# The scaling product of the feed-forward quantiser, moved from VectorE to GpSimd in two pieces, with the rounding as a step of its own

## The reference

```python
def _quantize_mx(x, ebits, mfrac, emax_elem, max_norm):
    xb = x.reshape(shp[:-1] + (shp[-1] // BLOCK, BLOCK))
    amax = jnp.max(jnp.abs(xb), axis=-1, keepdims=True)
    sexp = jnp.floor(jnp.log2(jnp.where(amax == 0, 1.0, amax))) - emax_elem
    sexp = jnp.clip(sexp, -SCALE_EMAX, SCALE_EMAX)
    scale = jnp.exp2(sexp)
    q = _quantize_elem(xb / scale, ebits, mfrac, max_norm) * scale
...
gate = _mx_linear(x, w_gate)
up = _mx_linear(x, w_up)
inter = jax.nn.silu(gate) * up
return _mx_linear(inter, w_down)
```

## Time and profile before

| | |
|---|---|
| median of three runs | 485.39 us (479.9, 485.39, 485.39) |
| the profiled execution: its time | 480.16 us |
| its span, first to last instruction | 478.3 us |
| mean granted TensorE clock, share of full speed | 0.921 |
| busy: TensorE, VectorE, ScalarE, GpSimd | 77%, 75%, 39%, 33% |

### The profile page before, as it was taken

How to read it: one execution, slowest core, us unless ns; L and a number is a source line. 1 busy time by engine, 2 the same in 40 slices (tenths; PEclk the granted TensorE clock), 3 DMA queues, 4 the chain that set the end, 5 groups by cost and what they waited for, 6 DMA issues and landing times.

```text
span 478.3 us, 6936 instructions
## 1 busy us (share of the span) xinstructions
PE 367.9 (77%) x2330; PEld 248.8 (52%) x2330; DVE 359.5 (75%) x857; ACT 188.4 (39%) x331; POOL 155.6 (33%) x147
## 2 busy tenths in 40 slices
PE   7899788999999678957948888977656488650764
PEld 4576456545568457846635565656533156430333
DVE  4588348685549999699796667569995986789895
ACT  4456427233232204412354354533005488540331
POOL 4019400087416325554325413123412110031240
PEclk9999999899999879999979999999888789976687
DMA  8900000032120222234973911824000760000001
GB/s 281 254 28 1 10 1 2 0 112 84 48 67 14 75 89 88 89 88 115 227 123 82 172 56 46 131 57 56 0 1 0 122 122 1 2 0 6 18 19 47
DMA packets 33713, 32.67 MB, mean 68 GB/s; under 512 B 3876, under 2 KB 32784, under 8 KB 33680
## 3 DMA queue, kind: packets, MB, share of 16 engines
q1 hardware_dynamic: 31088, 28.99, 26.1%
q0 software_dynamic: 992, 1.68, 1.1%
q10 hardware_dynamic: 1600, 1.57, 1.0%
HBM read 28.04 MB, written 4.19 MB: 67 GB/s over the span
## 4 chain that ended last, share of the span: by engine, by line
PE 45%; DVE 31%; issue 12%; ACT 8%; POOL 3%; DVEq 0%; ACTq 0%; POOLq 0%
PE bank L870 10%; PE bank L782 5%; PE bank L896 5%; PE bank L755 3%; PE bank L798 3%; PE bank L1006 2%; PE bank L970 2%; DVE mxraw L1624 2%; DVE x L1458 2%; DVE mam L1466 2%; DVE probs L1551 2%; PE bank L766 2%; PE bank L918 2%; PE bank L832 1%; ACT probs L1078 1%
## 5 line engine op out<-in xcount | busy, mean ns | idle before, releaser
L870 PE MATMUL bank<-tok_r,probs_r 128*128 128x512 f32 x104 | 46.6, 448 | 17.4 <-DVE wT L1447 9.7
L896 PE MATMUL bank<-wexp,wT 128*128 128x256 f32 x192 | 53.5, 403 | 6.0 <-DVE x L1458 5.9
L1128 ACT ACTIVATE silu_sb<-bank 128x512 f32<-128x512 f32 x32 | 19.1, 598 | 79.3 <-PE bank L870 79.3
L673 POOL TENSOR_TENSOR wexp_r<-wexp,probs_r 128x1024 fp32r<-128x1024 f32 x13 | 31.3, 2409 | 48.1 <-ACT probs_r L1089 48.1
L1325 DVE TENSOR_SCALAR probs<-probs,hi 128x512 f32<-128x512 f32 x64 | 35.0, 599 | 14.8 <-ACT probs L1078 14.7
L591 POOL TENSOR_TENSOR mx_grid<-parts,bl 128x1024 bf16<-128x1024 fp8e4 x9 | 17.2, 1908 | 88.5 <-DVE parts L1627 88.5
L1078 ACT ACTIVATE probs<-bank 128x1024 f32<-128x1024 f32 x32 | 32.2, 1026 | 29.8 <-PE bank L782 29.8
L896 PEld LDWEIGHTS bank<-wexp,wT 128*128 128x128 f32 x192 | 36.6, 200 | 13.1 <-issue 6.7
L1551 DVE SCALAR_TENSOR_TENSOR probs<-bank,dexp 128x384 f32<-128x384 f32 x48 | 26.5, 555 | 21.2 <-PE bank L956 15.3
L870 PE MATMUL bank<-tok_r,wexp_r 128*128 128x512 f32 x104 | 41.7, 401 | 0.0
L576 POOL TENSOR_TENSOR mxraw<-mxraw,mx_grid 128x512 f32<-128x512 f32 x12 | 15.3, 1278 | 69.6 <-DVE mx_grid L1492 69.6
(11 more groups left out here) (261 smaller groups left out, 891.1 us busy)
## 6 DMA issues: line engine op xcount, KB each, us to landing
wexp<-in_L_ffn_W SPq DMA_DIRECT2D x28, 256.0 KB, 4.0
krep<-part_dram SPq DMA_DIRECT2D x32, 128.0 KB, 5.3
qrep<-part_dram SPq DMA_DIRECT2D x32, 128.0 KB, 4.8
wexp<-in_L_ffn_Wg SPq DMA_DIRECT2D x14, 256.0 KB, 4.3
part_dram<-parts POOLq DMA_DIRECT2D x4, 384.0 KB, 3.0
part_dram<-parts SPq DMA_DIRECT2D x4, 384.0 KB, 2.6
x<-in_x ACTq DMA_DIRECT2D x2, 512.0 KB, 7.2
ctx<-in_ctx SPq DMA_DIRECT2D x2, 512.0 KB, 6.9
```

What stands on the lines that cost most here:

```text
L673: gp.tensor_tensor(low, raw, w_high[k % 2].bitcast(F32), ALU.subtract).then_inc(s["w_low_ready"], 1)
L870: mm = pe.matmul(bank[:, bk, :], lhs, rhs, start=(kk == 0 and q == 0), stop=(kk == KC - 1 and q == len(terms) - 1))
L896: mm = pe.matmul(bank[:, 2 + pair, D * t:D * t + D], hid[k % 2][m][:, col:col + P], wexp[:, k % WR, 2, m, :], start=(m == 0), stop=(m == 1))
L1128: act.activation(silu_sb[:, w % 2, :], bank[:, 0, :], ACT.Silu if direct else ACT.Tanh, scale=1.0 if direct else 0.5).then_inc(s["sigmoid_ ...
```

## The change

The multiplication with the inverse scale leaves VectorE. GpSimd does it, as two instructions over 512 columns each, once VectorE has signalled the inverse scale (new semaphore `q_inverse`); the second piece signals `q_scaled`. The rounding, which waits for that, and GpSimd's multiplication with the scale become a step `round` with a place of its own in the plan. In `stage_d` it stands between the first and the second `product` of the next stage. For quantise 0 it stands behind `accumulate` of steps 30 and 31.

```diff
-    plan += st("out", 30, 31) + st("quantise", 0) + st("accumulate", 30, 31)
+    plan += st("out", 30, 31) + st("quantise", 0) + st("accumulate", 30, 31) + st("round", 0)
...
-        return [now("last", 4, True) + early, part(0), part(1) + late, now("quantise", 0) + now("down", 3, True)]
+        return [now("last", 4, True) + early, part(0) + now("round", 1), part(1) + late, now("quantise", 0) + now("down", 3, True)]
...
             def quantise(k):
+                gp.wait_ge(s["q_inverse"], k + 1)
+                if k >= 1:
+                    gp.wait_ge(s["q_rounded"], k)
+                src = q_source(k)
+                for c in range(0, 1024, PIECE):
+                    m = gp.tensor_tensor(b3(q_tmp[:, c:c + PIECE]), b3(src[:, c:c + PIECE]), blocks(bl[:, k % 2, 2, c // 32:(c + PIECE) // 32]),
+                                         ALU.mult)
+                m.then_inc(s["q_scaled"], 1)
+
+            def round_(k):
...
-                seq.add(v.tensor_scalar(bl[:, b, 2, :].bitcast(I32), bl[:, b, 1, :].bitcast(I32), -1.0, float(0x7F000000 - (4 << 23)),
-                                        ALU.mult, ALU.add))
+                v.tensor_scalar(bl[:, b, 2, :].bitcast(I32), bl[:, b, 1, :].bitcast(I32), -1.0, float(0x7F000000 - (4 << 23)),
+                                ALU.mult, ALU.add).then_inc(s["q_inverse"], 1)
                 seq.add(v.tensor_scalar(bl[:, b, 3, :], bl[:, b, 1, :], 16.0, None, ALU.mult))
-                seq.wait()
-                seq.add(v.tensor_tensor(b3(q_tmp), b3(src), blocks(bl[:, b, 2, :]), ALU.mult))
+
+            def round_(k):
+                b = k % 2
+                v.wait_ge(s["q_scaled"], k + 1)
                 seq.wait()
                 lim = 7.5 / 64
                 v.tensor_scalar(q8[:, b, :], q_tmp, lim, -lim, ALU.min, ALU.max, saturate=False).then_inc(s["q_rounded"], 1)
```

More of the change, by code:

```diff
@@ L92 @@
 SPLIT_FROM = 3
+PIECE = 512
 SILU_STEPS = (3, 4, 5, 6, 7, 8, 14, 15)
@@ L405, in flamingo_layers @@
             e_done d_done qk_done c_done pvc_done pvc_copied t3_done h_placed h_centred h_squared h_scaled
-            mx_scaled q_rounded q_ready last_q_ready q_turned xqt_copied gu_done sil_done inter_ready it_copied dn_done x_final out_stored
+            mx_scaled q_inverse q_scaled q_rounded q_ready last_q_ready q_turned xqt_copied gu_done sil_done inter_ready it_copied dn_done x_final out_stored
             v_seq a_seq g_seq""".split()
@@ L691, in cell_in @@
                                  lsc[:, :].unsqueeze(1).broadcast_to([P, TH, D]), ALU.mult).then_inc(s["h_scaled"], 1)
-            steps = dict(w_split=w_split, x_split=x_split, mx_quantise=mx_quantise, q_split=q_split, cell_in=cell_in, quantise=quantise)
+            steps = dict(w_split=w_split, x_split=x_split, mx_quantise=mx_quantise, q_split=q_split, cell_in=cell_in, quantise=quantise, round=round_)
             for name, i in plan:
@@ L1647, in _ @@
                          cell_normalise=cell_normalise, cell_in=cell_in, cell_mid=cell_mid, cell_out=cell_out,
-                         quantise=quantise, product=product, last=last)
+                         quantise=quantise, round=round_, product=product, last=last)
             for name, i in plan:
```

## The result

In 20 runs of each kernel the change took the median from 484.86 to 487.85 us, 0.6% more. Ratios in this document are of the runs in the fast state alone, while the profiles of e5_round3_late, e8_one_piece, e10_round3_again and e12_before_again are of runs in a slow one, over 1.5% above the fastest of their kernel and with a granted clock of 0.883 to 0.894. The ratio is 1.0074, its 95% interval [1.0051, 1.0097]: 0.7% slower in this comparison. A second comparison of the same two kernels, with ten runs of the changed one (e4_again), gave medians of 487.38 against 485.89 us and a ratio of 0.9961 [0.9908, 1.0014]. So the timing settles that the difference is under 2%, and not how large it is or on which side. The forecast was 487 and +3.2 us (0.7%). The profiled execution took 486.79 us, its span is 485.1, its mean granted clock 0.909.

A forecast was written before the change was run, and what follows sets the result against it. VectorE's stream was taken to bound the tail, latency quantise 0, 4 and 9. Terms 0.86 + 0.50 - 0.31 + 0.86 + 0.41 + 0.86 gave +3.2 us; weighing 488.6 twice and 483.3 once gave 487, range 480.5 to 493.

The forecast's parts named there:

- Quantise 0, +0.86: At quantise 0, accumulate fills VectorE's wait, but the scale-back and all after it come 0.86 us later.
- Quantise 1 and 2, +0.50: In the middle, two exposed paths partly covered by each first product: 0.15 + 0.09 + 0.27, so +0.50 us.
- Quantise 3, -0.31: At quantise 3, a shorter lock wait gains 1.72 us; late rounding costs 0.61 and L1481's wait 0.81: -0.31 net.
- Quantise 4, +0.86: Latency-bound quantise 4 comes 0.86 us later; quantise 5's own path hides behind the wait for its successors.
- Quantise 6 to 9, +0.41: Three tail stages from quantise 6 to 9 take 16.71 us in place of 16.30: +0.41.
- the period of 5.57: Length in us of each tail stage after the change, as one loop through VectorE and GpSimd, with small gaps.
- The 0.09 of waiting: In each tail stage, L1481 would wait 0.09 us for the port lock held by GpSimd's scale-back.
- Quantise 9, +0.86: At quantise 9 nothing but a last is left to overlap, so the longer path costs 0.86 us.
- the lower price: Both GpSimd pieces at 1.91 us in place of 2.10, -0.19 at each of eight exposed places: sum +1.7 us.
- The relief counts: Rival, 7%: pieces hidden under other work, stages 1, 2, 5 to 8 each gain 1.26 us; about 480 us.
- TensorE's clock rises sooner: Rival, 15%: moved q_turn 3 and down 1 raise the clock before quantise 4's gate_up, saving 1.5 us: +1.7, 485.5.
- Slow pieces: Rival, 12%: each GpSimd piece takes 2.22 us, adding 2.3 at each of eight places: +22 us, 507.

The follow-up runs named there:

- e5_round3_late: Kernel before, every product still on VectorE, but quantise 3 rounded and scaled back late, behind cell_out and ahead of the last normalisation; ratio 0.9938 to the kernel before.
- e8_one_piece: Changed kernel with GpSimd's product as one instruction of 1024 columns in place of two of 512; ratio 1.0054 to the kernel before.
- e10_round3_again: Second run of the kernel before with only quantise 3 rounded and scaled back late, no product moved to GpSimd; ratio 0.9999 to the kernel before.
- e12_before_again: The kernel before itself, unaltered, profiled and timed once more; ratio 1.0016 to the kernel before.
- e1_front: Kernel before with the change made for quantise 0, 1 and 2 alone; ratio 1.0054 to the kernel before.
- e6_after_both: Changed kernel with the rounding put behind the second product of the next stage, so both products precede it; ratio 1.0109 to the kernel before.
- e3_tail: Kernel before with the change made for quantise 4 to 9 alone; ratio 1.0023 to the kernel before.
- e2_third: Kernel before with the change made for quantise 3 alone; ratio 0.9867 to the kernel before.
- e11_third_again: Second run of the kernel before with the change made for quantise 3 alone; ratio 0.9972 to the kernel before.

## Why the prediction was right, point by point

The forecast's sum was met by the first comparison (+3.2 against +3.0 between the medians and +3.29 over A, B and C). The second pair of profiles, e4_again against e12_before_again, has -0.87 in A, +0.07 in B and +1.33 in C, in all +0.53, and their medians differ by 1.5. So that the total came out to 0.2 us is luck. The mechanism held: longer paths at exposed places, and a saved 1.26 us of VectorE that turn mostly into waiting. The sizes of its points:

1. *Quantise 0, +0.86.* The path from L1633 to the rounding was 2.17 (356.54 to 358.71), with the `accumulate` steps in it as said; +0.79 by the same row of before.
2. *Quantise 1 and 2, +0.50.* Too much. From the maxima of quantise 1 to those of 2 came +0.07 for the 0.24 of the working (5.29 to 5.36), and from the inverse of quantise 2 to the end of the second product +0.18 for 0.27 (3.27 to 3.45). The rest of A lies within the spread of A, between 64.11 and 66.45 in the eight profiles whose front is unchanged (mean 65.36) and between 65.58 and 67.08 in the five with it changed (after, e1_front, e4_again, and with the variations of e6_after_both and e8_one_piece; mean 66.36). That is +1.0 where points 1 and 2 together said +1.36, with a spread that doesn't resolve it. Most of the +2.92 between the two first profiles is no sure part of the change; the part of the 0.70 clock above stays open.
3. *Quantise 3, -0.31.* Right in mechanism: L1580 waits for the second piece and L1481 for the late scale-back. But B gained 0.76, and where the cell values were slow it lost 0.07 to 0.12, which the point didn't allow for. In the first case all three of its terms were a little off, on the same side. L1582, behind the waiting L1580, starts 4.05 after the maxima in place of 5.98, so -1.93 where -1.72 was said. The late rounding lengthens the way from the last normalisation (L1278, L1265 before) to the maxima of quantise 4 from 1.41 to 1.89, +0.48 for +0.61. L1481 grew from 0.18 to 0.86, +0.68 for +0.81. Two of the three have one reason: a held tensor_scalar ends 0.03 to 0.04 after GpSimd's instruction (L1567 of before: 421.27 after 421.24; L1580: 425.75 after 425.71; L1481 in e6_after_both: 466.16 after 466.13). So its own 0.17 to 0.18 lie under the wait and don't follow it, as I had counted them.
4. *Quantise 4, +0.86.* From the inverse of quantise 4 to the maxima of quantise 6 it was 11.43 in both profiles of before, 11.96 after and 12.23 in e4_again: +0.53 to +0.80. Where this `gate_up` took 3.60 us on both sides, as in e4_again, the difference is +0.80; the 0.27 less is the clock's (below). Quantise 5's own path was hidden, as said.
5. *Quantise 6 to 9, +0.41.* This was wrong, in sign as well: 16.30 and 16.31 before, 16.09 after and in e4_again, -0.2. The step that failed is the period of 5.57. Measured it is 5.36, three times over in after and e4_again, and 5.35 to 5.37 in e3_tail. The 0.09 of waiting were not there: L604 ends at 462.99, L1481 starts at 462.89 and takes its usual 0.18. That fits the reason of point 3, by which so short a wait lies within the instruction. The path is 2.17 and not 2.24, and the "small gaps" were not there. Fully exposed, the stages are 0.2 shorter than VectorE's own stream was with a `last` in it (5.56, 5.57), and longer by 0.19 than the one without it (5.17). That "DVE's saved 1.23 us per stage turns wholly into waiting" is nearly right: in a stage with a `last` 1.09 of wait stand for the 1.26 of the product that went. In the stage without one the wait is 1.49, more than was saved.
6. *Quantise 9, +0.86.* From its maxima to the last `last` 9.27 before and 10.08 after, 9.74 and 10.50 in the second profiles: +0.81 and +0.76.

So the tail was put too high (+2.13, measured +1.13 and, between the second profiles, +1.33) and the gain at quantise 3 too low, by 0.45; and an excess in A that the points don't explain made up the rest. The total is right partly because its errors had both signs. The lower end of the range, 480.5, is also not what it was said to be: the lower price, +1.7, on 479.9 or 480.16 gives 481.6 to 481.9.

The rivals. *The relief counts* is out: the steps would have had to be near 4.3. *TensorE's clock rises sooner* is out as priced, 1.5 us, but not in kind. Quantise 4's `gate_up`, for which the earlier trace rows had a clock of 0.50, ran some 6.4 us later in the profile after, and its stretch there has 0.57:

```profile
451.50:455.00 3.50, 3.46 (x11) 1.39 (x12) 0.90 (x2) 0.68 (x2) 0.48 (x1) 0.57 0.05 16
```

Its eight matmuls took 3.34 us there and 3.60 in before and e4_again; the eight of `down` behind them 1.04, 1.92 and 1.37. That gave back 0.27 us in this execution and nothing in e4_again. In e2_third and e11_third_again, where `q_turn` 3 and `down` 1 stand nearer to it, 0.68 and 0.61 up to the maxima of quantise 6.

*Slow pieces* is out with 1.045 to 1.050 us for all twenty; beside them VectorE runs `last` and a `product`, which read one operand from PSUM. The range, 480.5 to 493, held the median.

## What to carry to other kernels

Work moved to an idle engine saves nothing where the moving engine then has too little to do under the hand-over: set the other engine's time plus both hand-overs (here 2.17 us) against what is left in the stream up to the first reader (here 1.1), and count exposed places, not busy time. A small instruction that may share ports with GpSimd is worth a look at where GpSimd's long ones stand, since it can be freed of the wait (1.21 to 0.17 us here, at the same slow cell values) without moving work at all. The stretch around it gave back only 0.15 to 0.35 us of that. And a term of one microsecond is read from stretches between fixed instructions in several profiles, as the whole time of one profile differs by more without any change.

## What the runs showed of the hardware that was not expected

- GpSimd's product of two f32 operands of 128 x 512, one of them a scale repeated over blocks of 32, took 1.047 us, and as 128 x 1024 1.912, while L578 with both operands in full takes 1.288 for 512. L578 is a subtraction, and so the operation differs too. But L690, a product of f32 operands that repeats nothing within a row of 256, took 2.36 and 2.39 us for 128 x 1024 in before, against 1.912. So the operand repeated over blocks of 32 is the cheaper one. The Trainium skill's page "GPSIMD Engine Reference", section "3.1 Elementwise — side-by-side cycle accounting", gives 4497 ns for an f32 tensor_tensor add of 2048 elements. As an estimate from that figure, 512 take 1.12 us; the traces have 0.07 less with the repeated operand and 0.17 more without.
- A tensor_scalar on VectorE of 16 or 32 columns, 0.17 to 0.18 us by itself, took up to 1.69 us beside one GpSimd instruction (L1567 beside L591), while a tensor_reduce of 1024 columns beside the same kind of instruction kept its 1.21 (L1479 beside L604 in e6_after_both).
- The maxima of quantise 0, ahead of which all kernels here have the same streams, lie at 351.11 to 361.35 us in fourteen profiles. The matmuls of the cell values took 1.51 us in some and 2.31 to 2.79 in others, with the kernel before among both (1.51, and 2.31 in its second profile).
- Ratios move by more than their intervals from one comparison to the next: the changed kernel had 1.0074 [1.0051, 1.0097] and in e4_again 0.9961 [0.9908, 1.0014]. The medians of the same two comparisons are 0.6% and 0.3% above the kernel before. The stretches carried this study, C above all, and the 0.7% rests on the larger comparison alone.
